# Statistics taken earlier and convolutions kept whole in the first phase of a decoder layer

## The reference

```
hs = layernorm(x)                                     # per row of 256: mean, variance
q = silu(dwconv(hs @ q_proj_w.T, q_conv_w))           # causal, depthwise, 4 taps
k = silu(dwconv(hs @ k_proj_w.T, k_conv_w))
v = silu(dwconv(hs @ v_proj_w.T, v_conv_w))
beta = sigmoid(hs @ b_proj_w.T)
delta = delta_rule(l2n(q), l2n(k), v, beta)           # chunks of 32 rows, in sequence
```

## Time and profile before

| | us |
|---|---|
| median of 3 runs | 1144.95 (1144.04 to 1145.99) |
| profiled execution, its own time | 1144.12 |
| its span, first to last instruction | 1142.3 |
| busy in the span: PE, DVE, ACT, POOL | 997.4, 803.6, 528.2, 622.9 |
| mean granted clock of TensorE | 0.95 |

### The profile page before, as it was taken

How to read it: one execution, slowest core, us unless ns; L and a number is a source line. 1 busy time by engine, 2 the same in 40 slices (tenths; PEclk the granted TensorE clock), 3 DMA queues, 4 the chain that set the end, 5 groups by cost and what they waited for, 6 DMA issues and landing times.

```text
span 1142.3 us, 26147 instructions
## 1 busy us (share of the span) xinstructions
PE 997.4 (87%) x9538; PEld 733.1 (64%) x9538; DVE 803.6 (70%) x2110; ACT 528.2 (46%) x992; POOL 622.9 (55%) x1009
## 2 busy tenths in 40 slices
PE   4899997887699899899999989989989999988991
PEld 2465657765476676576666667667667667767891
DVE  2879984543676866787677687687678775657487
ACT  2877774513333532542443443353253255755770
POOL 5469898438126636816816735653673215335562
PEclk9999998869799989999989999999999999999996
DMA  9444534450101250260161152122111173224589
GB/s 197 133 163 143 175 93 149 151 157 19 57 20 42 75 151 21 65 185 31 65 183 38 47 141 93 48 70 77 38 55 58 56 266 110 90 89 128 166 286 341
DMA packets 87100, 127.69 MB, mean 112 GB/s; under 512 B 28352, under 2 KB 62784, under 8 KB 84800
## 3 DMA queue, kind: packets, MB, share of 16 engines
q1 hardware_dynamic: 79776, 106.30, 30.2%
q0 software_dynamic: 7200, 19.74, 4.8%
HBM read 66.47 MB, written 59.55 MB: 110 GB/s over the span
## 4 chain that ended last, share of the span: by engine, by line
PE 45%; POOL 20%; DVE 20%; issue 8%; ACT 4%; DMA 1%; SPq 1%; ACTq 0%; DVEq 0%; POOLq 0%
POOL arena L1544 7%; POOL arena L1546 7%; DVE arena L1673 3%; PE bank L562 3%; PE bank L499 3%; PE bank L734 3%; PE bank L468 2%; PE bank L970 2%; POOL orn L1562 2%; PE bank L816 2%; POOL arena L1434 2%; PE bank L576 2%; PE bank L436 2%; PE bank L934 2%; PE bank L588 2%
## 5 line engine op out<-in xcount | busy, mean ns | idle before, releaser
L1044 ACT ACTIVATE arena<-bank 128x512 f32<-128x512 f32 (+4 forms) x358 | 185.9, 539 | 348.8 <-PE bank L961 61.8
L1544 POOL TENSOR_TENSOR arena<-arena 128x126 f32<-128x126 f32 (+22 forms) x248 | 107.0, 432 | 43.9 <-DVE arena L1732 26.1
L1673 DVE SCALAR_TENSOR_TENSOR arena<-arena,param 128x512 f32<-128x512 f32 x144 | 104.1, 777 | 18.8 <-ACT arena L1067 18.1
L1607 POOL DMA_INDIRECT results<-arena x78 | 76.3, 978 | 71.2 <-DVE arena L2225 42.9
L1546 POOL TENSOR_TENSOR arena<-arena 128x126 f32<-128x126 f32 (+22 forms) x248 | 102.2, 412 | 19.4
L419 PE MATMUL bank<-const,arena 128*128 128x128 f32 x256 | 40.5, 310 | 52.7 <-DVE arena L2162 26.7
L1489 POOL DMA_INDIRECT slots_x<-arena x64 | 63.6, 994 | 37.3 <-DVE arena L1964 21.4
L970 PE MATMUL bank<-arena 128*128 128x128 f32 x624 | 83.6, 277 | 0.2 <-ACT arena L1344 0.2
L1513 POOL TENSOR_TENSOR arena<-arena,rb 128x256 f32<-128x256 f32 x32 | 19.7, 616 | 116.5 <-ACT arena L1044 116.0
L970 PEld LDWEIGHTS bank<-arena 128*128 128x128 f32 x624 | 76.9, 194 | 0.4 <-issue 0.4
L1442 POOL COPY arena<-arena 32x128 f32<-32x128 f32 x128 | 53.5, 418 | 38.2 <-DVE arena L1722 31.4
(11 more groups left out here) (293 smaller groups left out, 2635.6 us busy)
## 6 DMA issues: line engine op xcount, KB each, us to landing
arena<-slots_x SPq DMA_DIRECT2D x78, 129.0 KB, 2.1
slots_x<-rows_of_no_token SPq DMA_DIRECT2D x8, 1161.0 KB, 11.7
xt<-x_in SPq DMA_DIRECT2D x16, 512.0 KB, 5.6
kq<-kq_T SPq DMA_DIRECT2D x8, 1024.0 KB, 9.0
arena<-results SPq DMA_DIRECT2D x32, 256.0 KB, 4.8
kq_T<-kq SPq DMA_DIRECT2D x7, 1024.0 KB, 3.9
arena<-ffn_in SPq DMA_DIRECT2D x7, 768.0 KB, 4.1
vT<-v_T SPq DMA_DIRECT2D x8, 514.0 KB, 4.0
```

Of the source, the lines that this page charges most:

```text
L1044: free(act.activation(out_, in_, func, **kw), name)
L1544: own.link(pool.tensor_tensor(tmp, rows32[:, m0:, k].unsqueeze(2).broadcast_to([P, nm, k]), units[:, 0:k, k].unsqueeze(1).broadcast_to([P, ...
L1607: pool.indirect_dma_start(results[:, :], bass.IndirectOffsetOnAxis(ap=dest[:, n % YS:n % YS + 1], axis=0), ys[:, n % YS, :], None).then_in ...
L1673: ins = V.scalar_tensor_tensor(cv[:, k % 4, :], pre[:, j, d:d + GT], param[:, at:at + 1], cv[:, k % 4, :], ALU.mult, ALU.add)
```

## The change

Two things change on VectorE; no other engine's program does.

The statistics of group i + 2 are taken in group i, behind convolution 3, where those of group i + 1 were taken at its start. Those of group 1 are still taken before the loop. The three taps of a convolution follow each other, each waiting for the one before it (`link` waits for the instruction just issued). Tap 3 of convolution 5 now stands before `front_units` in group 6.

```diff
-            def tap(i, j, d):
+            def conv(i, j):
                 k = 6 * i + j
-                if d == 1:
-                    dve.wait_ge(sem("first_tap"), k + 1)
-                else:
-                    after(tapped[k])
-                at = PARAM["conv"][0] + j * CONV + d
-                ins = V.scalar_tensor_tensor(cv[:, k % 4, :], pre[:, j, d:d + GT], param[:, at:at + 1],
-                                             cv[:, k % 4, :], ALU.mult, ALU.add)
-                if d < CONV - 1:
-                    tapped[k] = step(ins)
-                else:
-                    done(ins, "conv_ready")
+                dve.wait_ge(sem("first_tap"), k + 1)
+                at = PARAM["conv"][0] + j * CONV
+                for d in range(1, CONV):
+                    ins = V.scalar_tensor_tensor(cv[:, k % 4, :], pre[:, j, d:d + GT], param[:, at + d:at + d + 1],
+                                                 cv[:, k % 4, :], ALU.mult, ALU.add)
+                    if d < CONV - 1:
+                        link(ins)
+                    else:
+                        done(ins, "conv_ready")
...
+            hidden_stats(1)
             for i in range(NG):
-                if i + 1 < NG:
-                    hidden_stats(i + 1)
-                tap(i, 0, 1)
-                tap(i, 0, 2)
+                conv(i, 0)
                 if i == 0:
                     weights_scaled()
...
                 for j in range(1, 6):
-                    tap(i, j, 1)
-                    tap(i, j - 1, 3)
-                    tap(i, j, 2)
+                    conv(i, j)
                     if j == 2 and 3 <= i < 3 + T:
                         front_gram(0, i - 3)
+                    if j == 3 and i + 2 < NG:
+                        hidden_stats(i + 2)
                 if i == 2 + T:
                     front_units(0)
-                tap(i, 5, 3)
                 if i + 1 < NG:
                     dve.wait_ge(sem("conv_ready"), 6 * i + 6)
                     halo(i + 1)
```

More of the change, by code:

```diff
@@ L1662, in halo @@
                     done(V.memset(pre[:, :, 0:CONV - 1], 0.0), "halo_ready")
-            tapped = {}
-            def tap(i, j, d):
+            def conv(i, j):
                 k = 6 * i + j
-                if d == 1:
-                    dve.wait_ge(sem("first_tap"), k + 1)
-                else:
-                    after(tapped[k])
-                at = PARAM["conv"][0] + j * CONV + d
-                ins = V.scalar_tensor_tensor(cv[:, k % 4, :], pre[:, j, d:d + GT], param[:, at:at + 1],
-                                             cv[:, k % 4, :], ALU.mult, ALU.add)
-                if d < CONV - 1:
-                    tapped[k] = step(ins)
-                else:
-                    done(ins, "conv_ready")
+                dve.wait_ge(sem("first_tap"), k + 1)
[7 more added lines that the diff above has]
+                        done(ins, "conv_ready")
             def spread(i):
```

## The result

The change makes the kernel slower: 1151.98 us (median of 20 runs) against 1144.91 us (20 runs of the kernel before), a ratio of 1.0059 with a 95% interval of 1.0049 to 1.0070. The forecast was 1152.1 us and slower by 7.1 us; the medians differ by 7.07 us. The two profiled executions differ by more, 9.2 us in the span (1151.5 against 1142.3): 6.9 us of it up to the start of the long filters and 2.3 us behind them (963.7 against 961.4), where the diff touches nothing. In the profiled executions of all the kernels here, this last part takes between 961.4 and 966.5 us, though none of the edits reaches it.

A forecast was written before the change was run, and what follows sets the result against it. VectorE's own work, TensorE close behind, was taken to bound group 4, and a wait group 1. The group terms summed to +7.1 us, taking the median from 1144.95 to 1152.1 us; range 1146.0 to 1156.0.

The forecast's parts named there:

- The turn: Between groups VectorE must wait for ScalarE's first tap: the statistics fill a 1.94 us gap that stays when they go.
- The link: VectorE's taps: waiting for the tap just before costs 0.11 us (0.07 to 0.13); ten more per group, 1.1 us.
- rival 1: All 48 convolutions: a waiting tap costs no more than a waiting-free one; 1142.9 us, not slower; chance 0.12.
- The terms: Groups 0 to 7, shifts from last tap to last tap: +0.9, -2.1, +0.3, +2.9, +2.9, +2.5, -1.4, +1.1 us.
- The term for group 6: To group 7's first tap: waits of 1.66 and 0.3 us and SiLU (0.54) go, links add 1.1: -1.4 us.
- The term for group 7: Last group of the first phase: only the links of one-by-one convolutions count, +1.1 us.
- the dependent step of 0.95 us: Beside GpSimd's solve: a tap lasts 0.918 us, so a dependent step would be 0.95 against 0.83 interleaved.
- The wait of group 1: VectorE's 5.0 us wait, from late statistics through GpSimd, TensorE and ScalarE, goes; 1.81 + 1.1 come: -2.1 us.
- Rival 2: Groups 1 to 6: taps step quicker away from GpSimd's rows, 1.1 us a group back; 1145.6, no change; chance 0.08.
- Rival 3: Groups 1 and 2: late row loads start the statistics 1 to 2 us late; +3, 1155; chance 0.10.
- Rival 4: Group 1: GpSimd still gets its statistics late, so the chain through TensorE and ScalarE stays; no size or chance given.

The follow-up runs named there:

- leaving the statistics out: Statistics of groups 2 to 7 left out of the kernel before: 1138.44 us, ratio 0.9963; left out of the changed kernel: 1142.71 us, ratio 0.9994.
- the statistics alone: Kernel before with only the statistics of group i + 2 moved behind projection 3's taps, taps still interleaved: 1143.99 us, ratio 0.9999.
- whole convolutions alone: Kernel before with only the convolutions done one by one, statistics still at the start of a group: 1144.12 us, ratio 1.0006.
- the versions that take them two groups ahead: Kernel before with statistics two groups ahead at the turn, rows loaded one group earlier, taps interleaved: 1150.54 us, ratio 1.0064; two variants followed.
- one group of eight: Kernel before with the convolutions of group 1 alone done one by one: 1140.43 us, ratio 0.9968.
- one statistic early: Kernel before with group 2's statistics alone taken in group 0 behind projection 3's taps, all taps interleaved: 1145.70 us, ratio 1.0003.
- the version two groups ahead with whole convolutions: Kernel before with statistics two groups ahead at the turn, rows loaded one group earlier, convolutions one by one: 1157.63 us, ratio 1.0115.
- GpSimd's changed order: Interleaved version with statistics two groups ahead at the turn, GpSimd now normalizing the next rows before the diagonals: 1145.92 us, ratio 1.0019 to the kernel before.

## Why the prediction was right

**The turn.** Right, and the key step. The gap of 1.94 us at the turn from group 2 to 3 stayed to the hundredth, and leaving the statistics out showed it from both sides: no gain in groups 4 and 5 where they fill the turn, 1.5 to 1.8 us a group where they stand in the middle.

**The link.** Ten more links a group were put at 1.1 us; they measured 1.09 to 1.21 in groups 1 to 5. The rule in the Trainium skill, "VectorE: DVE Perf Modes", "Rules for kernel authors", that one should save instructions and not semaphores, does not hold for these taps: rival 1, links free, fell with the statistics alone at 1143.99 us (0.9999) and both at 1151.98 us (1.0059).

**The terms**, forecast and measured (fourth row of the table less the first): group 0 +0.9 and +0.9; group 1 -2.1 and -2.2; group 2 +0.3 and +0.25; groups 3, 4 and 5 +2.9, +2.9, +2.5 and +3.05, +2.6, +2.65; group 6 -1.4 and -0.8; group 7 +1.1 and -0.2. The measured sum is +6.3, the forecast one +7.1. That the medians differ by 7.07 is chance to that extent: the 0.8 us between lie within what single executions vary by ahead of the first tap and behind the long filters. The term for group 6 was off by 0.6 us. Both waits and the SiLU went as forecast (1.66, 0.27 and 0.50 us), but the rest of the group, its taps above all, got about 1.7 us longer and not 1.1: the nine behind the grams took 7.25 us, where nine take 6.74 to 6.81 in groups 0 to 2. They run beside GpSimd's copies of the diagonals; whether that is the reason was not tested. The term for group 7 was mis-sized: 1.1 us, and nothing measured. Its steps beside GpSimd's solve were 0.83 us interleaved, and (12.40 - 0.8) / 14 = 0.83 one by one. The taps there are shorter when one by one. All taps of group 7, shortest, median and longest in ns, first with the statistics alone (interleaved), then in the changed kernel:

```profile
L1673 DVE SCALAR_TENSOR_TENSOR arena<-arena,param x18: 670/894/978, 160.2 to 175.9; 128x512 f32<-128x512 f32 x18
```

```profile
L1669 DVE SCALAR_TENSOR_TENSOR arena<-arena,param x18: 668/808/952, 168.1 to 184.0; 128x512 f32<-128x512 f32 x18
```

So the dependent step of 0.95 us, which I had worked out from the interleaved median, was not there.

**The wait of group 1.** Here the number was right and the account incomplete. I took the 5.0 us for the work of the statistics' place alone. It was made by that place, by GpSimd's rows, which took 7.44 us beside interleaved taps, and by TensorE's stretch at half clock behind its pause; whole convolutions alone remove nearly as much of it (3.2 us) as the statistics alone (3.4). The forecast came out because in the full change the wait can only go once. This is where the sum of the halves fails: in groups 3 to 5 the prices add up (4.8 us and 3.9 us alone, 8.3 together), in group 1 the gains do not (-3.4, -3.2, together -2.2). In groups 0, 2 and 6 both together come out 1.2 to 1.5 us longer than the halves add up to. Hence 0, +1 and +7 us.

**The other rivals.** Rival 2, quicker taps away from the rows: in the changed kernel the rows take 6.0 us instead of 6.5, but no group shows the 1.1 us of the rival. Rival 3, a new wait in the middle: none in the changed kernel. A wait of the statistics for GpSimd did appear in the versions that take them two groups ahead. Rival 4, a ring that is not broken: the statistics of group 2 ended at 38.10 us, before group 1 began, and TensorE did not pause for its rows.

## What to carry to other kernels

Before work is moved out of its place in an engine's queue, look whether the engine would stand still there without it; work in such a gap is free, and between instructions that do not wait it costs nearly its length (1.5 to 1.8 of 1.81 us here). When two edits cure the same wait, each may look harmless or good alone, and together their prices add while the cure counts once: time each alone and both. An order that is denser on one engine can go with slower work on another beside it (rows of 7.44 us against 5.80 here), so the looser order belongs only where the slowed one is on the chain: here one group of eight, 0.9968 of the time before.

## What was not expected of the hardware

GpSimd's normalization of four tiles of 128x256 took 4.8 us ahead of the first tap, where VectorE stands idle, and 5.8 to 5.9 us beside the taps in every group of the kernel whose convolutions alone go one by one. Beside interleaved taps it took 6.4 to 6.7 us in most groups of the kernel before, and 7.4 to 8.1 us in the group that holds the long wait, there and with one statistic early. The order of the taps is not all that counts: in the changed kernel it was 6.0 us, in two groups of the version two groups ahead with whole convolutions 6.8, and in GpSimd's changed order, beside interleaved taps, up to 7.8 without the long wait. What the trace shows to be different between the two orders is a step of 0.79 us between taps of one convolution instead of 0.66 to 0.72; that this step is the reason is argued, not shown. In the other direction, taps beside GpSimd's solve had a median of 894 ns interleaved and 808 ns one by one, at the same step of 0.83 us. What the two engines share was not measured.
